# Two attentions: exponentials split into f16 halves, turned by DMAs, and multiplied with f16 halves of the values

## The reference

```python
x = x + tanh(g_xattn[0]) * L0_xattn(layernorm(x), ctx, ctx, mask, wq, wk, wv, wo, bq, bk, bv, bo)
x = x + tanh(g_ffn[0])   * L0_ffn(layernorm(x), ...)      # 64 experts, top 8, and a shared one
x = x + tanh(g_xattn[1]) * L1_xattn(layernorm(x), ctx, ctx, wq, wk, wv)
x = x + tanh(g_ffn[1])   * L1_ffn(layernorm(x), ...)      # fused experts with a running sum

def L0_xattn(query, key, value, mask, ...):               # 16 heads of 32
    q = (query @ wq.T + bq); k = (key @ wk.T + bk); v = (value @ wv.T + bv)   # split into heads
    scores = einsum('bhqd,bhkd->bhqk', q, k) / sqrt(32)
    scores = clip(scores, -100, 100); scores = where(mask == 0, -inf, scores)
    attn = softmax(scores, axis=-1)
    return einsum('bhqk,bhkd->bhqd', attn, v) @ wo.T + bo
# L1_xattn: the same without mask, clip, biases and wo
```

## Time and profile before

| | us |
|---|---|
| median of 3 runs | 2781.3 (2780.76 to 2789.81) |
| the profiled execution, its own time | 2809.87 |
| its span | 2808.1 |
| one block of the first attention (228.09 to 277.61) | 49.5 |
| one block of the second attention (1769.91 to 1809.80) | 39.9 |

### The profile page before, as it was taken

One profiled execution on the slowest core, in us unless ns is written; L12 is line 12 of the kernel. 1 busy time (PEld: TensorE's weight loads), 2 busy tenths in 40 slices (PEclk: granted clock), 3 DMA queues, 4 the chain that ended last, 5 costly groups with the idle time before them and its releaser, 6 DMA issues. The chain is left out here.

```text
span 2808.1 us, 44981 instructions
## 1 busy us (share of the span) xinstructions
PE 2644.7 (94%) x16990; PEld 1473.8 (52%) x16990; DVE 1594.4 (57%) x2629; ACT 1425.9 (51%) x3586; POOL 1042.0 (37%) x823
## 2 busy tenths in 40 slices
PE   5999988999999989999999979999999999999999
PEld 3554544444444457777777645565444444444444
DVE  6888885655555346655656568988543422333222
ACT  3888885323222146666666548999443222322221
POOL 1455451465555636666766500111102201221111
PEclk8999999999999999999999989999999999999999
DMA  6221214222222269999999842321420110011000
GB/s 186 52 85 57 74 31 169 61 61 61 75 70 54 76 215 289 285 296 282 288 288 289 207 101 76 91 44 42 157 64 16 46 42 34 16 46 46 19 12 30
DMA packets 287479, 311.17 MB, mean 111 GB/s; under 512 B 155169, under 2 KB 164129, under 8 KB 287265
## 3 DMA queue, kind: packets, MB, share of 16 engines
q1 hardware_dynamic: 250400, 240.96, 27.0%
q0 software_dynamic: 36864, 67.34, 11.7%
HBM read 198.86 MB, written 75.89 MB: 98 GB/s over the span
## 5 line engine op out<-in xcount | busy, mean ns | idle before, releaser
L1376 POOL DMA_INDIRECT ids<-sh_tk,sh_su x256 | 269.8, 1054 | 243.9 <-PE sh_gu L55 70.5
L55 PE MATMUL ex_gu<-ex_xT,ex_h 128*128 128x256 f16 x3072 | 347.5, 273 | 4.6 <-issue 3.8
L55 PEld LDWEIGHTS ex_gu<-ex_xT,ex_h 128*128 128x128 f16 x3072 | 301.2, 98 | 53.9 <-issue 4.4
L1775 POOL DMA_INDIRECT xp<-ex_oo,ex_to x128 | 242.3, 1893 | 178.6 <-ACT ex_oo L1683 123.2
L2323 POOL TENSOR_TENSOR fe_prodT<-fe_pp,fe_prodT 128x512 f16<-128x512 f32 x64 | 77.5, 1210 | 591.2 <-ACT fe_prodT L2108 591.2
L521 PE MATMUL at_g<-id,at_p 128*128 128x128 f32 x1280 | 205.1, 288 | 38.7 <-POOL at_p L901 30.7
L1510 DVE SCALAR_TENSOR_TENSOR ex_h<-ring,ex_h 128x1024 f16<-128x1024 f32 x128 | 151.1, 1222 | 153.0 <-ACT ex_h L1500 153.0
L521 PEld LDWEIGHTS at_g<-id,at_p 128*128 128x128 f32 x1280 | 164.9, 169 | 106.9 <-issue 41.7
L680 ACT ACTIVATE at_s<-at_s,at_mx 128x154 f32<-128x154 f32 x512 | 210.4, 417 | 0.0
L900 POOL TENSOR_TENSOR at_p<-at_s,at_rs 128x1024 f32<-128x1024 f32 x64 | 121.5, 1898 | 223.3 <-DVE at_rs L800 223.3
L55 PE MATMUL at_g<-hm_zT,hm_w 128*128 128x512 f16 x768 | 182.1, 389 | 19.8 <-issue 12.5
(11 more groups left out here) (331 smaller groups left out, 5407.8 us busy)
## 6 DMA issues: line engine op xcount, KB each, us to landing
ring<-L_ffn_expert_gate_up_w SPq DMA_DIRECT2D x64, 1024.0 KB
ring<-L_ffn_expert_down_w SPq DMA_DIRECT2D x64, 512.0 KB
ring<-x SPq DMA_DIRECT2D x24, 1024.0 KB, 5.8
x<-ring SPq DMA_DIRECT2D x16, 1024.0 KB, 4.7
zrows<-hm_zs SPq DMA_DIRECT2D x32, 256.0 KB
xp<-ring SPq DMA_DIRECT2D x8, 1024.0 KB
out<-ring SPq DMA_DIRECT2D x8, 1024.0 KB, 4.3
ring<-xp SPq DMA_DIRECT2D x7, 1024.0 KB, 5.7
```

The source lines that it names most:

```text
L55: mm = nc.tensor.matmul(out, lhs(a, k), rhs(b, k), start=start and i == 0 and j == 0, stop=stop and i == n - 1 and j == 2)
L1376: e.indirect_dma_start(ids, bass.IndirectOffsetOnAxis(slotu[b % 2][:, t, j:j + 1], 0), pair[b % 2][:, t, j, :], None, bounds_check=SLOTS - ...
L1775: e.indirect_dma_start(dst, bass.IndirectOffsetOnAxis(to[:, n:n + 1], 0), o32[y % 2][:, t, :], None, bounds_check=T + SLOTS - 1, oob_is_er ...
```

## The change

Exponentials stay in f32 in `at_s`. Their f16 high half is made by ScalarE in the first attention and by VectorE in the second (`high`), the low half (the rest) by GpSimd in both. Each half is turned by one DMA transpose that SyncE issues (`turn_keys`, 128x1280 f16 = 320 KB) straight into `at_pT`, which now has two halves. The 10 transposes and the three copies a unit are gone. The values are kept in two f16 halves as well, and the product is a sum of three f16 products (high by high, high by low, low by high).

In the first attention the row sums and the multiplication by their reciprocals are gone. TensorE multiplies both halves with matrices of ones (`each`, `every`) into another bank `d`; ScalarE takes exp(-ln(d)) of it, VectorE multiplies it with the product, ScalarE casts to the f16 high half (piece `halves`, at the end of the step) and GpSimd makes the low half, after everything else in its step. GpSimd also makes the low halves of the normalised rows (but for the first block). In the second attention the copy of half of the scores is gone (three pairs of PSUM banks rotate for scores) and the general banks go from four to two; `values` moves from 8b+6, 7, 10, 11 to 8b+7, 7, 11, 11.

The diff, cut to its core:

```diff
+        gen = [ps(f"g{i}", [P, 512]) for i in range(4 if L0 else 2)]
+        S = ps("S", [P, HH, 256])
+        pairs = [S[:, HG * i:HG * i + HG, :] for i in range(2)]
+        if not L0:
+            pairs.insert(0, maps_ahead.gen[:, :, :].rearrange("p b (k n) -> p (b k) n", n=256))
+
+        def scores(i, part):
+
+            return pairs[(2 * i + part) % len(pairs)]
...
-        VR = [sb(f"VR{g}", [P, KT, P], F32) for g in range(BATCH)] if L0 else A.VR
+        V = [sb(f"V{g}", [P, 2, D], F16) for g in range(BATCH)] if L0 else A.V
-        sc = [sb(f"s{i}", [P, HH if L0 else HG, CTX], F32) for i in range(NS)]
-
-
-        prob = [sb(f"p{i}", [P, HH * (P + HD)], F32) for i in range(NP)]
-        pT = [sb(f"pT{i}", [P, HH + 2, BLK], F32) for i in range(2)]
-        mx, sm = ([sb(f"{n}{i}", [P, HH], F32) for i in range(3)] for n in ("mx", "sm"))
+        sc = [sb(f"s{i}", [P, HH, CTX], F32) for i in range(NS)]
+
+
+        prob = [sb(f"p{i}", [P, 2, HH * (P + HD)], F16) for i in range(NP)]
+        pT = [sb(f"pT{i}", [P, 2, HH + 2, BLK], F16) for i in range(2)]
...
-        VALS, FIN = ((7, 8, 11, 12), (13, 13, 14, 14)) if L0 else ((6, 7, 10, 11), (12, 12, 13, 13))
+        VALS, FIN = ((7, 8, 11, 12), (13, 13, 14, 14)) if L0 else ((7, 7, 11, 11), (12, 12, 13, 13))
...
-        rank = dict(split_ahead=0, low=0, turn=2, prepare=3)
+        rank = dict(split_ahead=0, low=0, turn=2, prepare=3, halves=4)
...
-                    e.wait_ge(s["p_act"], by_scalar * unit)
-                    e.wait_ge(s["p_vec"], (3 - by_scalar) * unit)
-                    out = bank(("o", n), (s["o_lo" if L0 else "o_hi"], n + 1))
+                    for i in range(unit - NP, unit):
+                        e.wait_ge(*keys_landed(i))
+                    out = bank(("o", n), (s["o_div" if L0 else "o_hi"], n + 1))
                     ptb = pT[(2 * B + u) % 2]
                     grp = 2 * u + gi
-                    for j in range(HG):
-                        o = grp * P + j * HD
-                        e.matmul(out[j * HD:(j + 1) * HD, :], V[g][:, o:o + HD], ptb[:, place(gi * HG + j), :],
-                                 start=True, stop=False)
-                    e.matmul(out[:, :], VR[g][:, grp, :], ptb[:, HH + gi, :], start=False, stop=True).then_inc(s["o_mm"], 1)
+                    heads = [(slice(j * HD, (j + 1) * HD), place(gi * HG + j)) for j in range(HG)]
+                    for hv, hp in TERMS:
+                        for rows, k in heads:
+                            o = grp * P + rows.start
+                            e.matmul(out[rows, :], V[g][:, hv, o:o + HD], ptb[:, hp, k, :],
+                                     start=(hv, hp) == TERMS[0], stop=False)
+                    for hv, hp in TERMS:
+                        mm = e.matmul(out[:, :], VR[g][:, hv, grp, :], ptb[:, hp, HH + gi, :], start=False,
+                                      stop=(hv, hp) == TERMS[-1])
+                    mm.then_inc(s["o_mm"], 1)
+                    if L0:
+                        out = bank(("d", n), (s["d_ln"], n + 1))
+                        for hp in range(2):
+                            for rows, k in heads:
+                                e.matmul(out[rows, :], each[:, :], ptb[:, hp, k, :], start=hp == 0, stop=False)
+                        for hp in range(2):
+                            mm = e.matmul(out[:, :], every[:, :], ptb[:, hp, HH + gi, :], start=False, stop=hp == 1)
+                        mm.then_inc(s["d_mm"], 1)
...
-                i = n - behind
-                if 0 <= i < UNITS:
-                    e.wait_ge(*((s["prob"], i + 1) if L0 else (s["expd"], 2 * i + 1)))
-                    keys_turned(i, 0, 0)
-                for what in plan[n][:1]:
+                for what in plan[n]:
                     piece(*what)
...
+                    if L0:
+                        if n == 0:
+                            e.wait_ge(s["v_mm"], 2 * BATCH)
+                        elif n >= 2:
+                            e.wait_ge(s["o_div"], n - 1)
+                        e.wait_ge(s["d_mm"], n + 1)
+                        e.activation(recip[n % 2], bank_of["d", n][:, :], ACT.Ln).then_inc(s["d_ln"], 1)
+                        e.wait_ge(s["d_ln"], n + 1)
+                        e.activation(recip[n % 2], recip[n % 2], ACT.Exp, scale=-1.0).then_inc(s["d_inv"], 1)
+                        return
...
+                elif what == "halves":
+                    u, gi = k
+                    n = 4 * B + 2 * u + gi
+                    if (u, gi) == (0, 0) and B:
+                        e.wait_ge(s["f_mm"], TPB * B)
+                    e.wait_ge(s["o_div"], n + 1)
+                    e.copy(oT[:, 0, 2 * u + gi, :], o32[n % 2]).then_inc(s["o_hi"], 1)
...
+                    to = sc[i % NS][:, k, :]
+                    if L0:
+                        x = e.activation(to, to, ACT.Exp, bias=mx[i % 3][:, k:k + 1])
+                    else:
+                        x = e.activation(to, scores(i, part)[:, h, 0:CTX], ACT.Exp, bias=mx[i % 3][:, k:k + 1],
+                                         accum_out=sm[i % 3][:, k:k + 1])
...
-            def part_copy(i, part):
+            def high(i):
+
...
+                e.wait_ge(s["expd"], 2 * i + 2)
+                if i >= NP:
+                    e.wait_ge(*keys_landed(i - NP))
+                if i == 0:
+                    e.wait_ge(s["blank"], NP)
+                e.copy(first_keys(prob[i % NP][:, 0, :]), sc[i % NS][:, :, 0:P])
+                e.copy(last_keys(prob[i % NP][:, 0, :]), rest_of(i)).then_inc(s["p_hi"], 1)
...
+                    exps(n - lag, part)
+                    if part and L0:
+                        high(n - behind)
+                    for what in plan[n]:
+                        if (what[0] == "values") == (part == 0):
+                            piece(*what)
...
-                    nm.vector_low(n)
+                    if not (L0 and B):
+                        nm.vector_low(n)
...
+                    if n >= 2:
+                        e.wait_ge(s["o_hi"], n - 1)
+                        e.wait_ge(s["o_lo"], n - 1)
+                    e.wait_ge(s["o_mm"], n + 1)
+                    e.wait_ge(s["d_inv"], n + 1)
+                    e.tensor_tensor(o32[n % 2], bank_of["o", n][:, :], recip[n % 2], ALU.mult).then_inc(s["o_div"], 1)
...
+                if not L0:
+                    high(n - behind)
+                for what in plan[n]:
+                    piece(*what)
...
+                elif what == "low" and L0 and B:
+                    nm, _, n = whose(B, k)
+                    nm.low(e, n)
+                elif what == "halves":
+                    u, gi = k
+                    n = 4 * B + 2 * u + gi
+                    e.wait_ge(s["o_hi"], n + 1)
+                    e.tensor_tensor(oT[:, 1, 2 * u + gi, :], o32[n % 2], oT[:, 0, 2 * u + gi, :], ALU.subtract
+                                    ).then_inc(s["o_lo"], 1)
...
+                if 0 <= n - behind < UNITS:
+                    i = n - behind
+                    rows = prob[i % NP]
+                    e.wait_ge(s["p_hi"], i + 1)
+                    e.tensor_tensor(first_keys(rows[:, 1, :]), sc[i % NS][:, :, 0:P], first_keys(rows[:, 0, :]), ALU.subtract)
+                    e.tensor_tensor(last_keys(rows[:, 1, :]), rest_of(i), last_keys(rows[:, 0, :]), ALU.subtract
+                                    ).then_inc(s["p_lo"], 1)
                 for what in plan[n]:
                     piece(*what)
+            e.wait_ge(s["p_lo"], UNITS)
             if L0:
...
+            def turn_keys(i):
+
+                if i % TPB == 0 and i // TPB >= 2:
+                    e.wait_ge(s["o_mm"], 2 * (i // TPB) - 2)
+                t = i % TPB
+                for h, made in enumerate(("p_hi", "p_lo")):
+                    e.wait_ge(s[made], i + 1)
+                    e.dma_start_transpose(pT[i // TPB % 2][:, h, :, t * P:(t + 1) * P], prob[i % NP][:, h, :]
+                                          ).then_inc(s[f"keys{i % NP}"], 16)
```

254 lines of the change are left out of this document (105 added, 149 removed).

## The result

The changed kernel took 2933.3 us (median of four runs, 2929.3 to 2941.9) against 2785.6 before: 1.053 times as long, 95% interval 1.049 to 1.057. Forecast was 2817 within 2745 to 2862. The sign was right, the size was not.

What follows compares the result with a forecast made beforehand. TensorE and its handovers with VectorE and ScalarE were taken to set both attentions' periods, at full clock. First attention +32 and second +4 gave +36 on the median of 2781.3: 2817 us, range 2745 to 2862.

Steps and rivals of the forecast that it cites:

- +57 for +32: First attention: forecast 32 us slower, 28 over seven seams between blocks and 4 at its end.
- the +4 chosen: First attention's block: 4 us longer at each of 7 seams, range +2.5 to +6.5.
- The working: First attention's closed loop once a block: three parts sum to 53.4 us against 49.5, or 56 with the low clock.
- the discount: First attention's clock loss: taken midway between none and the full 2.9 us a block, less the scores' slack.
- (a): First attention's loop, from step 4's high half through GpSimd's low halves to the output's low half: 6.6 us.
- the 2.9 of the clock: First attention: 24 matmuls after idling take 8.25 us instead of 5.34 at half clock, adding 2.9 a block.
- (c): First attention's loop on ScalarE, from step 7's logarithm to step 4's high half: 32.4 us.
- 28 + 4: First attention: 28 us over seven seams between blocks, plus 4 for serial work at its end.
- +72 for +4: Second attention: forecast 4 us slower, blocks +2, first blocks winning 3, the end losing 4 to 5.
- Rival 2: Second attention: clock stays low throughout, 43 us a block, whole kernel 2838 to 2860; chance 0.13.
- Rival 1: First attention's loop closes early at full clock: blocks 48.5 and 36.5, whole kernel 2754 us; chance 0.27.
- Rival 3: First attention: two at_p buffers make high halves wait for turns, +40 to +50, about 2860 us; chance 0.07.

Runs made afterwards that it cites:

- e1: Changed kernel, output's halves made earlier in the first attention, VectorE's scaling earlier in the second: 2887.7 us, kernel before 2782.5 on that chip.
- e2: Changed kernel, VectorE making normalised rows' low halves (first attention), row turns issued before exponentials' turns (second): 2904.6 us, kernel before 2782.5.
- e5: Changed kernel with the edits of e1 and e2 together: 2861.9 us, kernel before 2788.9 on that chip; blocks 48.1 and 47.4.
- e7: Changed kernel plus 36 extra matmuls while TensorE waits for the output's low half in the first attention: 2926.4 us, kernel before 2788.9.
- e9: e5 with the next stage's loads issued behind the first attention's last turns of exponentials: 2874.3 us, kernel before 2813.4 on that chip.
- e10: e9 plus 14 extra matmuls before each block's first Q product in the second attention: 2863.4 us, kernel before 2813.4 on that chip.
- e3: Changed kernel with only the exponentials' high halves turned, products using them for the low ones: 2913.9 us, kernel before 2782.5.
- e6: e5 with only the exponentials' high halves turned, products using them for the low ones: 2838.6 us, kernel before 2788.9.
- e4: Changed kernel with four general banks and two score pairs in the second attention, for two and three: 2947.6 us, kernel before 2782.5.
- e12: e9 with four general banks and two score pairs in the second attention: 2896.6 us, kernel before 2813.4 on that chip.
- e13: e12 with VectorE's copy of half of the scores out of PSUM restored: 2885.0 us, kernel before 2812.2 on that chip.

## Why the prediction was wrong

**The first attention, +57 for +32.** The mechanism and its place were right, and e1, e2 and e5 show it by taking it away. The term that was mis-sized is the block, +7.0 for the +4 chosen. The working had 53.4, and 56 with the clock; measured are 56.5. Two steps failed. One is the discount: "I take the middle between no loss and this, less what the scores' slack gives". There was no slack to give: the low clock cost the product 2.2 a block in the mean, and in e7 what of it came back, 0.8, shortened the period by 0.7. The other is in (a): 8.2 for 6.6, since the output's cast on ScalarE stands behind casts of rows that VectorE can't supply before GpSimd has made its low halves. The sum followed GpSimd's order and not ScalarE's at the same step. That the 56 worked out with the clock came so near is in part luck: the 2.9 of the clock and the 32.4 of (c) were too much, and the 1.6 that (a) lacked made up for it.

**Its ends.** By the stores of its blocks the first attention lost 9.6 before the first, 35.0 in five blocks, 6.7 and 11.4 in the last two, 62.6 together, for 28 + 4 (the +57 above is read before the last product's tail). The start was in no term; with e5's orders its first store comes 2 us later than before instead of 9.6, so it is mostly the same loop. Of the end, the loads in front of the last turns, worth 3 to 5 by e9, were in no term either: a turn's issue and landing were priced, what its queue held in front of it was not.

**The second attention, +72 for +4.** The step that failed is "The Q product of step 4 waits for a bank that VectorE frees by its scaling (0.74 each), four in a row behind unit work: 2 to 3; steps 5 and 6: 1.8 and 1.0". The wait was the one named, but it took 8.1 at step 4 and 2.1 at the next. The sum counted VectorE's unit work before the scaling (maxima, reciprocal, high half, 2.3 us in the timeline) and left out what the table puts there as well, the rows: 5.0 of the 8.1, partly because single instructions of lines 148 and 166 took about four times as long beside a GpSimd that now works. Further, the turns of rows have one buffer, which the last Q product frees, and share SyncE's queue with turns of exponentials: TensorE's 4.4 us before the next block's first product. The forecast weighed this by sums only ("SyncE about 32 ... Neither is the bound"). And the exponentials hold the scores' banks in PSUM, whose price (four waits, 8.9 us a block with three pairs) appeared nowhere. Rival 2, the clock, had 43 and was given 0.13: the low clock did come, but costs 1 to 2 by e10, and 3.6 if all Q matmuls are counted.

**The rivals.** Rival 1 (faster) had named the point from which it decides, a first attention's block under 49.5. e5 reaches 48.1, near its 48.5, once the orders are changed, so what it took for granted was the order. Its 36.5 for the second attention is far from all versions. Rival 3 (the ring of two buffers) didn't come: ScalarE waited 0.6 us in all for a landed turn, in the whole attention. The DMA engines were busy 42 to 44 us a block for the 34 to 35 worked out; with half of the turns gone the first attention didn't move, and the second moved by 2.5 to 2.8 (e3, e6).

**What stays open.** Of the second attention's +11.1, orders account for about 4, turns 1 to 3, the clock 1. The rest, 3 to 5, moves between waits for two banks, for exponentials and for VectorE with each layout (e4, e12, e13). A lack of PSUM banks is part of it at most, since e13 has the banks and the copy of before and 46.7. VectorE's slow instructions beside GpSimd are the rival that no run tested: none took GpSimd's low halves away and left the rest. It can't be all either: the last three blocks, which prepare no rows, still lost 6.0, 4.2 and 13.1. No run showed 40 with the change's arithmetic.

**The high half, and the clock without transposes.** Where GpSimd is idle the high half took 0.64 + 0.26 = 0.90 us in the change, and this is its mean too, under the 1.2 that was taken. By the Trainium skill, page "VectorE: DVE Perf Modes", section "The perf-mode tier table (the rule you actually need)", it was to cost about 0.7 us, an estimate; the trace's 0.90 is near it. The second attention's clock fell to 0.83 in the mean of a block. By the Trainium skill, page "TensorE: Matmul & The Clock Gate", section "Part 4: PE-mode transpose", taking transposes away would have left it its clock. TensorE also idled 21 of 51 us there, so the runs don't separate the two.

## What to carry to other kernels

When an edit moves a piece to another engine, walk each queue at the step in which the piece's result is due and sum everything that stands in front of it, on every engine of the chain; busy sums of a block don't show it. Price what stands there at its duration beside the newly busy engine, not at the one it has today. A bank or buffer's price is the time until the last instruction that frees it, and where a copy is taken away, what it freed early is held longer. Once a closed loop is found, its low clock belongs in it whole; don't average it away.

## What was not expected of the hardware

TensorE's clock: behind 36 matmuls at full clock and a pause of 2.1 us it was granted 1.00 when work returned in two blocks and 0.50 in a third (e7); after 3.5 us it was 0.50 both times, and after 0.5 to 1.9 us behind 14 matmuls it was full in four blocks (e10).

A 320 KB turn costs more than 1.25 times a 256 KB one: the DMA engines were busy 42 to 44 us a block for 34 to 35 scaled by size. Half of the turns, eight a block, are worth the step from 0.89 to 0.55 over 340 us between e5 and e6, about 2.0 us each, where 1.45 was scaled. The issue of one on SyncE took 1.35 us in the median, and ten in a row kept SyncE 17.6 in e5.

VectorE beside GpSimd: in the second attention a low half of a row (line 166) took 0.68 or 2.54 us and a row (line 148) 0.52 to 0.79 or 2.29. The high half of 1024 columns took 0.64 when GpSimd was idle and up to 1.66 beside it, that of 208 columns 0.26 and up to 1.33. The maxima (line 883) took 0.77 to 0.80 either way.
